# Causal and local attention masks as TensorE matmuls, and global attention in nine full-width units

## What is computed

```python
def sdpa(q, k, v, mask):
    scores = jnp.einsum('bhqd,bhkd->bhqk', q, k) / np.sqrt(HD).astype(np.float32)
    scores = jnp.where(mask, scores, jnp.float32(-1e+30))
    probs = jax.nn.softmax(scores, axis=-1)
    return jnp.einsum('bhqk,bhkd->bhqd', probs, v)
# global: causal = i[:, None] >= i[None, :]
# local:  diff = i[:, None] - i[None, :]; mask = (diff >= 0) & (diff < WIN)     (WIN = 32)
```

## Time and profile before

| | |
|---|---|
| median of 3 runs | 1610.28 us (1608.38 to 1612.85) |
| the profiled execution: its own time | 1602.86 us |
| the profiled execution: span of the profile | 1601.0 us |
| mean granted TensorE clock | 0.886 |
| PE busy | 1241.3 us (78%) |
| DVE busy | 1047.1 us (65%) |
| ACT busy | 869.9 us (54%) |
| POOL busy | 384.7 us (24%) |

### The profile page before, as it was taken

How to read it: one execution, slowest core, us unless ns; L and a number is a source line. 1 busy time by engine, 2 the same in 40 slices (tenths; PEclk the granted TensorE clock), 3 DMA queues, 4 the chain that set the end, 5 groups by cost and what they waited for, 6 DMA issues and landing times. The chain is left out here.

```text
span 1601.0 us, 35341 instructions
## 1 busy us (share of the span) xinstructions
PE 1241.3 (78%) x14546; PEld 743.6 (46%) x14546; DVE 1047.1 (65%) x1732; ACT 869.9 (54%) x1337; POOL 384.7 (24%) x559
## 2 busy tenths in 40 slices
PE   1479997385235999747715999999999999999985
PEld 0323334354132333335512666666666666666662
DVE  5633334798574333468856677777777777777755
ACT  1368885352225888635413556555556555565541
POOL 1100000243110000014334443343333333443320
PEclk7679999577566999976857999999999999999997
DMA  2032210250002222005213111011011010110101
GB/s 57 6 74 54 54 27 1 73 140 1 28 0 53 53 54 53 1 20 139 54 38 97 29 26 29 19 28 26 22 26 28 19 29 22 25 29 20 27 12 53
DMA packets 32868, 61.86 MB, mean 39 GB/s; under 512 B 9248, under 2 KB 15168, under 8 KB 32704
## 3 DMA queue, kind: packets, MB, share of 16 engines
q1 hardware_dynamic: 32704, 59.55, 15.2%
HBM read 7.90 MB, written 2.10 MB: 6 GB/s over the span
## 5 line engine op out<-in xcount | busy, mean ns | idle before, releaser
L587 ACT ACTIVATE att_probs<-psum 128x1024 f32<-128x1024 f32 (+2 forms) x480 | 364.6, 823 | 117.4 <-PE psum L484 110.0
L1258 POOL TENSOR_TENSOR ffn_rot<-ffn_rot,ffn_rot_sin 128x512 f32<-128x512 f32 x128 | 160.2, 1273 | 397.9 <-DVE ffn_rot L1285 397.9
L458 PE MATMUL psum<-att_probs,att_v 128*32 128x512 f32 (+5 forms) x2688 | 225.1, 440 | 21.4 <-DVE att_ht L722 17.7
L484 PE MATMUL psum<-att_q_stack,att_k_stack 32*128 32x160 f32 (+4 forms) x1280 | 193.3, 420 | 57.9 <-ACT att_probs L587 29.9
L484 PEld LDWEIGHTS psum<-att_q_stack,att_k_stack 32*128 32x128 f32 x1280 | 98.9, 212 | 226.5 <-ACT att_probs L587 172.4
L747 DVE TENSOR_TENSOR att_probs<-att_probs,att_causal_mask 128x512 f32<-128x512 f32 x128 | 88.3, 690 | 167.9 <-ACT att_probs L587 166.3
L943 PE MATMUL psum<-ffn_w_qkv,xs 128*128 128x512 f32 x256 | 129.4, 629 | 25.8 <-PEq L849 23.5
L131 POOL TENSOR_TENSOR att_refine<-att_root 128x160 f32<-128x160 f32 x8 | 7.1, 887 | 504.4 <-ACT att_root L533 504.4
L326 DVE TENSOR_TENSOR att_probs<-att_probs,att_local_mask 128x480 f32<-128x480 f32 (+1 forms) x144 | 103.2, 779 | 10.2 <-ACT att_probs L587 10.2
L1076 PE MATMUL psum<-ffn_hn,ffn_w 128*128 128x512 f32 (+1 forms) x192 | 104.1, 629 | 6.6 <-ACT ffn_hn L1215 5.4
L1282 DVE TENSOR_TENSOR ffn_rot_sin<-psum,ffn_sin 128x1024 f32<-128x1024 f32 x64 | 78.2, 1222 | 46.1 <-ACT ffn_sq L1159 45.7
(11 more groups left out here) (176 smaller groups left out, 2391.5 us busy)
## 6 DMA issues: line engine op xcount, KB each, us to landing
att_k_stack<-att_k_parts SPq DMA_DIRECT2D x128, 128.0 KB, 2.6
ffn_v_back<-ffn_v SPq DMA_DIRECT2D x120, 130.0 KB, 2.4
att_q_stack<-att_q_hi SPq DMA_DIRECT2D x64, 128.0 KB, 2.6
att_q_stack<-att_q_lo SPq DMA_DIRECT2D x64, 128.0 KB, 2.8
xres<-in_hidden SPq DMA_DIRECT2D x4, 512.0 KB, 3.8
out<-out_y SPq DMA_DIRECT2D x4, 512.0 KB, 3.2
ffn_w_qkv<-in_f_wqkv SPq DMA_DIRECT2D x2, 768.0 KB, 7.3
ffn_w<-in_f_w SPq DMA_DIRECT2D x1, 682.0 KB, 5.7
```

What stands on the lines that cost most here:

```text
L458: ins = T.matmul(psum[32 * head:32 * head + V_PAD, (4 + cc) * BANK + lo - cc * BANK: (4 + cc) * BANK + hi - cc * BANK], v[:, e, kt, g * V_ ...
L484: ins = T.matmul(psum[:, base:base + width], k_stack[rows, g % 2, kt * P:(kt + 1) * P], q_stack[rows, g % 2, q0:q0 + width], start=True, s ...
L587: act.activation(probs[:, (unit0[a] + n) % E_BUFS, 2 * j:2 * j + 2, 0:width], ps2((step % 2) * 2).rearrange("p (h c) -> p h c", h=2)[:, :, ...
L1258: steps.did(pool.tensor_tensor(out, out, halves(k.rot_sin[:, n % 2, :])[:, :, 1 - half, :], ALU.add), g["added"] if half else None)
```

## The change

There are three parts.

1. **Units of the global stage.** `GLOBAL_UNITS` replaces `GLOBAL_ORDER`: narrow pieces are put side by side, so that a head group has nine units that are all 512 wide: (tile 0 of the first half), (tiles 3 and 1 of it), (tile 2 of it with tile 6 of the second half), then tiles 0, 1, 2, 3, 4 of the second half, and (tiles 7 and 5 of it). There are 18 score steps and exps for a head group instead of 24. The columns are the same 4608, and so are the numbers of score and value matmuls.
2. **Causal mask.** The multiplication on the DVE is gone. In each step of a unit that has a diagonal tile, PE adds behind the scores a matmul per bank, of the 128x128 identity in bf16 (`ident_bf`) with a bf16 table that is 0 or -1e30 (`causal_bf`), into the same PSUM. Five of the nine units have diagonals: one 128-wide block in two of them, one 256-wide in two, and two of 128 in one.
3. **Local mask.** The multiplications on the DVE and on POOL are gone. In each step PE first writes the mask with `ident_bf` and `local_bf` (as wide as the unit) into both banks, and the score matmuls add to it (`start=False`).

The two bf16 tables are made once by two DVE instructions in `prepare`, which loads one copy of the local mask instead of three.

```diff
...
+                c.did(nc.vector.tensor_scalar(keep.local_bf[:], widen(local_seen[:], [P, 3, SPAN_A]), -1.0, -HIDDEN,
+                                              ALU.add, ALU.mult))
+                c.did(nc.vector.tensor_scalar(keep.causal_bf[:], widen(keep.causal_mask[:], [P, 2, P]), -1.0, -HIDDEN,
+                                              ALU.add, ALU.mult))
...
-    GLOBAL_ORDER = ([0, 3, 2, 1], [0, 7, 6, 5, 4, 3, 2, 1])
+    GLOBAL_UNITS = (((0, 0),), ((3, 0), (1, 0)), ((2, 0), (6, 1)), ((0, 1),), ((1, 1),), ((2, 1),), ((3, 1),),
+                    ((4, 1),), ((7, 1), (5, 1)))
+    GLOBAL_OPENS, GLOBAL_CLOSES = (0, 6), (2, 5)
...
                 if a == 0:
-                    for c in range(S // CHUNK):
-                        for kt in GLOBAL_ORDER[c]:
+                    for tiles in GLOBAL_UNITS:
+                        pieces, at = [], 0
+                        for kt, c in tiles:
                             q0 = max(kt * P, c * CHUNK)
-                            out.append((e, g, [(kt, q0, (c + 1) * CHUNK - q0, 0, c)]))
+                            pieces.append((kt, q0, (c + 1) * CHUNK - q0, at, c))
+                            at += (c + 1) * CHUNK - q0
+                        out.append((e, g, pieces))
...
-            for n in range(len(UNITS[1])):
-                pool.wait_ge(exp_done, step0[1] + (n + 1) * STEPS)
-                mask_window(pool, n, DVE_HEADS).then_inc(masked_rest, 1)
...
-                    if is_masked(a, UNITS[a][n]):
-                        pe.wait_ge(masked, masked_before[a][n] + 1)
-                    if a == 1:
-                        pe.wait_ge(masked_rest, n + 1)
...
+                            banks = [((step % 2) * 2 + i) * BANK for i in range(2)]
+                            if a == 1:
+                                for i in range(2):
+                                    T.matmul(psum[:, banks[i]:banks[i] + width_of(pieces)], keep.ident_bf[:],
+                                             flat(keep.local_bf[:])[:, 0:width_of(pieces)], start=True, stop=True,
+                                             skip_group_check=True)
                             for kt, q0, width, at, ch in pieces:
                                 for i in range(2):
                                     rows = slice(32 * (2 * j + i), 32 * (2 * j + i + 1))
-                                    base = ((step % 2) * 2 + i) * BANK + at
-                                    ins = T.matmul(psum[:, base:base + width], k_stack[rows, g % 2, kt * P:(kt + 1) * P],
-                                                   q_stack[rows, g % 2, q0:q0 + width], start=True, stop=True)
+                                    ins = T.matmul(psum[:, banks[i] + at:banks[i] + at + width],
+                                                   k_stack[rows, g % 2, kt * P:(kt + 1) * P],
+                                                   q_stack[rows, g % 2, q0:q0 + width], start=a == 0 and at == 0,
+                                                   stop=True, skip_group_check=True)
+                            if a == 0:
+                                blocks = diagonals(UNITS[0][n])
+                                for block in ([] if not blocks else
+                                              [(0, 2 * P)] if blocks == [0, P] else [(at, P) for at in blocks]):
+                                    for i in range(2):
+                                        base = banks[i] + block[0]
+                                        ins = T.matmul(psum[:, base:base + block[1]], keep.ident_bf[:],
+                                                       flat(keep.causal_bf[:])[:, 0:block[1]], start=False, stop=True,
+                                                       skip_group_check=True)
...
-                    if is_masked(a, UNITS[a][n]):
-                        dve.wait_ge(exp_done, step0[a] + (n + 1) * STEPS)
-                        if a == 1:
-                            for head in range(DVE_HEADS):
-                                c.did(mask_window(V, n, head), masked if head == DVE_HEADS - 1 else None)
-                        else:
-                            buf = probs[:, (unit0[a] + n) % E_BUFS, :, :]
-                            c.did(V.tensor_tensor(buf[:, :, 0:P], buf[:, :, 0:P],
-                                                  widen(keep.causal_mask[:], [P, GROUP, P]), ALU.mult), masked)
...
```

More of the change, by code:

```diff
@@ L148, in prepare @@
         sig = k.sb("sig", [D, B])
+        local_seen = k.sb("local_seen", [P, 1, SPAN_A])
         loads = [
@@ L156, in prepare @@
             (keep.norm_w[:], dram["norm_w"]),
-            (keep.rope_a[:], dram["rope_a"]), *[(keep.local_mask[:, i:i + 1, :], dram["local_mask"]) for i in range(3)],
+            (keep.rope_a[:], dram["rope_a"]), (local_seen[:], dram["local_mask"]),
             (keep.causal_mask[:], dram["causal_mask"]),
@@ L253, in attention_pair @@
     scores_done, exp_done, pv_done = sem("scores"), sem("exp"), sem("pv")
-    masked, masked_rest = sem("masked"), sem("masked_rest")
     ot_copied, o_in_psum, o_ready = sem("ot_copied"), sem("o_s"), sem("o_ready")
@@ L272, in attention_pair, with opens_bank @@
     CHUNK = BANK
-    GLOBAL_ORDER = ([0, 3, 2, 1], [0, 7, 6, 5, 4, 3, 2, 1])
+    GLOBAL_UNITS = (((0, 0),), ((3, 0), (1, 0)), ((2, 0), (6, 1)), ((0, 1),), ((1, 1),), ((2, 1),), ((3, 1),),
+                    ((4, 1),), ((7, 1), (5, 1)))
+    GLOBAL_OPENS, GLOBAL_CLOSES = (0, 6), (2, 5)
     LOCAL_GROUPS = ((0, 1, 2), (3, 4, 5), (6, 7))
     def closes_bank(a, kt, cc):
-        return kt == (GLOBAL_ORDER[cc][-1] if a == 0 else 4 * cc + 3)
+        return kt == (GLOBAL_CLOSES[cc] if a == 0 else 4 * cc + 3)
+    def opens_bank(a, kt, ch, cc):
+        if a == 0:
+            return kt == GLOBAL_OPENS[cc] and ch == cc
+        return kt == (0, 3)[cc]
     def units(a):
@@ L295, in units, with diagonals @@
         return out
+    def diagonals(unit):
+        return [at for kt, q0, width, at, ch in unit[2] if q0 == kt * P]
     UNITS = [units(0), units(1)]
@@ L302, in attention_pair @@
     n_heads = PAIR * KV_HEADS
+    units_per_head = [len(UNITS[a]) // n_heads for a in range(2)]
     steps_per_head = [STEPS * len(UNITS[a]) // n_heads for a in range(2)]
@@ L306, in width_of @@
         return pieces[-1][3] + pieces[-1][2]
-    def is_masked(a, unit):
-        return a == 1 or unit[2][0][1] == unit[2][0][0] * P
-    masked_before = [[sum(is_masked(i, u) for i in range(a) for u in UNITS[i]) +
-                      sum(is_masked(a, u) for u in UNITS[a][:n]) for n in range(len(UNITS[a]))]
-                     for a in range(2)]
-    def opens_bank(a, kt, ch, cc):
-        return (kt == 0 and ch == cc) if a == 0 or cc == 0 else kt == 3
-    DVE_HEADS = 3
-    def mask_window(engine, n, head):
-        pieces = UNITS[1][n][2]
-        width = width_of(pieces)
-        row = probs[:, (unit0[1] + n) % E_BUFS, head, 0:width]
-        return engine.tensor_tensor(row, row, flat(keep.local_mask[:])[:, 0:width], ALU.mult)
     row = lambda e, i: widen(mod[:, e, i * D:(i + 1) * D].rearrange("p (o d) -> p o d", o=1), [P, TILES, D])
@@ L472, in _ @@
                         e, g, pieces = UNITS[a][n]
-                        if pieces[0][0] == 0 and (a == 1 or pieces[0][4] == 0):
+                        if n % units_per_head[a] == 0:
                             turn = a * n_heads + e * KV_HEADS + g
@@ L788, in attention_half @@
         keep.rope_a = k.sb("rope_a", [P, 2, 2, TILES, HEAD_DIM])
-        keep.local_mask, keep.causal_mask = k.sb("local_mask", [P, 3, SPAN_A]), k.sb("causal_mask", [P, 1, P])
+        keep.local_bf, keep.causal_mask = k.sb("local_bf", [P, 3, SPAN_A], BF16), k.sb("causal_mask", [P, 1, P])
+        keep.causal_bf = k.sb("causal_bf", [P, 2, P], BF16)
         keep.silu = k.sb("silu", [D, B])
```

1 line of the change is left out of this document (added).

## The result

| | before | after |
|---|---|---|
| median of 4 runs | 1610.42 us (1608.38 to 1612.85) | 1634.61 us (1631.13 to 1637.42) |
| ratio, with its 95% interval | | 1.0149 [1.0123, 1.0174] |
| profiled execution: own time, span | 1602.86, 1601.0 us | 1633.31, 1631.5 us |
| mean granted clock | 0.886 | 0.895 |

The change makes the kernel 24 us slower. Between the two profiled executions the change is 30.5 us of span, and the stages say where it went. A global stage is counted from its first score to ACT's first copy behind it, a local stage from its first score or mask to the same copy. "At 0.50" is how much of that time had a granted clock of 0.50, that is 1.2 GHz.

The account below looks back on a forecast made before the run. PE was taken to bound masked global units and, replacing the DVE, the local stage. +10 us global and +17 local made +27, so 1630 for the profiled execution and, with 7.4 more, a median of 1637 us; range 1595 to 1676.

Parts of the forecast that it names:

- the ring of 1.98 us: Global stage: PE and ACT hand work over in a 3.97 us cycle covering two units, 1.98 us per unmasked 512-wide unit.
- Masked global units, 2.26 and 2.53 us: Global stage, PE-bound: a unit takes 2.26 us with 128-wide masks, 2.53 with 256 columns of masks in two pieces.
- The global stage as a whole, +10 us: Global stage: a head group takes 21.2 us against 20.62, sixteen of them adding 10 us in all.
- Local units, 2.95 us for 480 columns: Local stage at full clock: PE needs 1.75 us scores and values, 0.80 masks, 0.40 shape changes per 480-wide unit.
- The local stage, +8.6 a pair: Local stage: 73.8 us of head groups, 6.5 slow clock, 2.1 tail, 82.4 us against 73.8; +17 us in all.
- From the sum to the median: Whole kernel: 1630 us for the profiled execution, plus 7.4 because the median of the runs lies higher, gives 1637.
- Weight loads exposed: Rival, both stages: each mask matmul also shows its weight load, 109 ns; 1660 to 1694 us, chance 0.17.
- The upper bound: Whole kernel: exposed loads add 2.4 us per global and 1.2 per local head group, +38 and +19 on +27, 1694.
- Shapes change for nothing: Rival, the two steps of a masked unit: array shape changes cost nothing, only streaming; down to 1591 us, chance 0.24.
- The clock comes at once: Rival, local stage start: denser work lifts the 17 us at 1.2 GHz, 2 x 6.5 us less, 1624; chance 0.06.
- scores 0.79 + a new way of 0.2 + the masks: Local 480-wide unit: two score steps at 0.79 us, one new change to the full array at 0.2, four masks at 0.20.
- the 0.65 us for two 512-wide steps: Global stage: PE's time for two back-to-back score steps, split into 0.22 and 0.43, with 0.2 for a shape change.

Follow-up runs that it names:

- Units alone: The changed kernel's nine full-width units kept, causal mask back on the DVE, local masks back on DVE and POOL; 1575.98 us, ratio to before 0.9799.
- the kernel with the other order: Changed kernel with PE masks ahead of the first step's scores and behind the second's, so both score steps stand side by side; 1588.54 us.
- causal mask alone: Kernel before with only the causal mask moved to PE: twelve old units, local stage as before; 1689.33 us, ratio 1.0494.
- local mask alone: Kernel before with only the local mask moved to PE: twelve old units, causal multiplication on the DVE; 1632.14 us, ratio 1.015.
- narrow masks: Changed kernel with every mask matmul cut to 16 columns, same places and full-array shape; 1603.14 us, ratio 0.9958.

## Why the prediction was right

The forecast was 1637 us for a measured 1634.6, slower by over 0.3%. Step by step:

- **Plain units, the ring of 1.98 us.** Right. "Units alone" has 18.94 us a head group where the sum of 9 x 1.98 and the transposes gives 19.0, with all eight multiplications still on the DVE. So taking them off it was worth nothing in this stage.
- **Masked global units, 2.26 and 2.53 us.** Measured 2.28 and 2.61. The head group came to 21.39 instead of 21.2. PE bounds it, as said.
- **The global stage as a whole, +10 us.** It was 8.4. The periods gave +0.77 x 16 = 12.3 us; 3.6 us less a stage at 0.50 took some 4 of it back. I had put nothing down for that.
- **Local units, 2.95 us for 480 columns.** Measured 2.96, a head group 8.96 for 9.2. The bound changed from DVE to PE.
- **The local stage, +8.6 a pair.** Measured +9.8 and +9.2, by two misses that cancel in part. Eight head groups at full clock would take 71.7 us and not 73.8, because a back transpose ahead of a mask takes 0.49 us and not 0.61. The rest of the stage is 11.9 us and not 8.6, because the stretch at 0.50 was 21.6 us and not the 17.3 that I carried over the earlier trace rows. Later dips went, as assumed.
- **From the sum to the median.** This was partly luck. The sum gave 1630 for the profiled execution, which took 1633.31: its span grew by 30.5 us and not by 27. I then added 7.4, the distance of the profiled execution before from its median; the one after lies only 1.3 below its own.
- **Weight loads exposed.** Fell. They take 99 ns each in the changed kernel and lie beside other work: a pair of 128-wide masks with the way back takes 0.21 us, one load more for each of the two would make it 0.4. With 16 columns the pair takes 0.14 (202.76 to 202.90), less than two loads one behind the other. The upper bound was also summed low: 24 and 12 loads of 109 ns are 2.6 and 1.3 us, which puts it some 5 us above 1694.
- **Shapes change for nothing.** Fell. With 16-column masks a head group still pays 1.13 us over "units alone".
- **The clock comes at once.** Did not happen: 13.4 and 21.7 us of the stages stood at 0.50. The time at 0.50 did move, in both directions.

**What the sum had wrong inside right totals.** I put each step's price down to two things, streaming and the change of shape. There is a third, the overlap of two neighbouring steps, and I had it in neither row: the 0.79 us that I took for two steps side by side must have held a wait, since with the masks moved outside the same twelve matmuls take 0.52. The trace of before could have told me. The row is 0.86 us long, and others of the same twelve matmuls there, like this one, are as short as the 0.58 of the kernel with the other order:

```profile
337.64 0.58 PE L484 MATMUL psum<-att_q_stack,att_k_stack 32*128 32x160 f32 x12
```

The step that failed is "scores 0.79 + a new way of 0.2 + the masks": the masks' price in a 480-wide unit is not 1.20 us (2.95 - 1.75) but 1.48 (2.96 - 0.52 - 0.96), and 0.47 of that is due to where they stand. The total hid this, because 0.79 and 0.2 is also 2 x 0.50. That is the main reason why my later expectations for order and placement were about half of what came; the time at 0.50, which also fell in those kernels, is the other. In the same way the 0.65 us for two 512-wide steps is a figure with a wait in it; they need 0.44. One of them alone needs 0.43, so the split of the pair into 0.22 and 0.43, and the 0.2 us for a change of shape that came from it, are shown by no run.

The rule of the Trainium skill (TensorEngine Tiling (Array Packing), Tiling Modes, Key Properties) that a change of tiling mode drains the engine agrees with the runs: with 16-column masks a masked unit still takes PE 0.69 us more, drain and lost overlap together, and a head group pays 1.13 us for five of them. The same list of the Trainium skill says that tiles work independently; the 0.52 us of two steps against 0.50 of one agrees. What I failed to do was to read the two together. The 81 ns that the Trainium skill gives (TensorE: Matmul & The Clock Gate, Back-to-back issue gap) would have made the total 1641; the head group missed by 0.19 us in that direction, but the traces do not tell issue from shape there.

**Open.** Why the time at 0.50 at a stage's start is 11 us in one kernel and 47 in another was not tried by itself. In the rows PE is nearly always busy during it, in the changed kernel for 21.60 of 21.60 us and in "causal mask alone" for 46.41 of 47.60, so gaps on PE as a whole do not explain it. Nor did full busy times keep the clock up: with 16-column masks it fell again in the middle of the local stage (352.91 us), after 27.3 us at full clock with PE busy for 26.3, and stayed at 0.50 for 20.5 us with PE busy for all of them. Within one execution the same code differs too: "local mask alone" has 20.6 us at 0.50 in its first local stage and 30.9 in its second. Some 3 us outside the stages, in parts whose code is the same, were not followed up either.

## What to carry to other kernels

Where matmuls use separate strips of the array, their neighbours run beside each other, and a full-array matmul between them costs that overlap as well as its own time; put such extra matmuls where the shape changes anyway, or give them the same strips. Read the price of a pair from a place where nothing waits inside it. Before work moves from one engine to another, split the change: here one part gained 33 us and the masks took 59 back, 46 of them by their order alone.

## What was not expected of the hardware

- Two steps of two heads, each head in its own 32 rows, take 0.44 us for 512 columns and 0.52 for 480 in three pieces; one such step takes 0.43 and 0.50. Four strips work as fast as two.
- With each mask in the strip of its head the first scores start 0.04 us after the first mask (335.80 to 335.84), with the pair on the full array 0.50 us after it (338.06 to 338.56). The same number and width of masks then costs a unit's two steps 1.02 us instead of 2.00.
- Less work on PE was not less time at 1.2 GHz. With 16-column masks the local stage stood at 0.50 for 41.5 us, with full ones for 21.7, with the same masks in the better order for 11.3. It goes with some 22 us of "causal mask alone" and about 20 of "narrow masks", the largest things that my sums left out.
